# Up weights turned on VectorE in phase A, merges cut in halves, and a shorter LoRA set-up in a one-core AdaLN + FFN kernel

## The reference

```python
# block 0: a per-sample 64x64 mixing, then a linear layer with 8 LoRA adapters summed into it
y  = einsum('bct,bcd->bdt', x, L0_cond_weights[itok_B_0_15])
x1 = x + (y @ W.T + bias + lora_out(y))            # lora: B (scaled by 2*lora_weights) times A, rank 8*16 = 128
# block 1: per-sample adapter of rank 16, then a gated FFN with 4-bit weights
x2 = (x1 @ B[id].T) @ A[id].T
Wg, Wu, Wd = NF4[codes] * scales                    # codes are int32, one scale per 64 inputs
out = x1 + (silu(x2 @ Wg.T) * (x2 @ Wu.T)) @ Wd.T   # hidden size 2752, i.e. 21 chunks of 128 and a tail of 64
```

## Time and profile before

| | us |
|---|---|
| median of 3 runs (1006.99 to 1011.08) | 1008.95 |
| the profiled execution, its own time | 1010.47 |
| its span, first to last instruction | 1008.8 |
| TensorE busy | 987.7 |
| VectorE busy | 878.0 |
| ScalarE busy | 775.0 |

### The profile page before, as it was taken

The page is one execution under the profiler, slowest core; times in us unless marked ns, Lnnn a source line. Parts: engine busy times, 40 slices in busy tenths (PEclk is TensorE's granted clock), DMA queues, the critical chain, the costliest instruction groups (busy, mean ns, idle before and its releaser), DMA issues.

```text
span 1008.8 us, 14537 instructions
## 1 busy us (share of the span) xinstructions
PE 987.7 (98%) x5280; PEld 845.6 (84%) x5280; DVE 878.0 (87%) x853; ACT 775.0 (77%) x929; POOL 231.3 (23%) x269
## 2 busy tenths in 40 slices
PE   4999999999999989999999999999999999999998
PEld 3898889889898868888888888888888888888887
DVE  3899999989999979999999999999999999962353
ACT  4788888878878869988988879888888888853220
POOL 4024533432441221122121211112302122121000
PEclk9999999999999999999999999999999999999999
DMA  9846447347334336866555555656366564564666
GB/s 245 221 139 155 99 110 173 87 104 192 86 93 98 69 58 125 147 116 129 104 101 106 97 101 120 112 105 126 84 122 112 101 120 88 106 136 76 194 221 230
DMA packets 73655, 126.28 MB, mean 125 GB/s; under 512 B 7505, under 2 KB 49505, under 8 KB 73585
## 3 DMA queue, kind: packets, MB, share of 16 engines
q0 software_dynamic: 15200, 51.41, 31.4%
q1 hardware_dynamic: 57056, 72.89, 24.4%
q10 hardware_dynamic: 1328, 1.05, 0.3%
HBM read 66.61 MB, written 67.11 MB: 133 GB/s over the span
## 4 chain that ended last, share of the span: by engine, by line
PE 89%; DVE 8%; DMA 1%; issue 1%; ACT 1%; ACTq 0%; DVEq 0%
PE ps_z L1157 23%; PE ps_y L1157 23%; PE ps_z L1011 13%; PE ps_gu L1136 12%; PE ps_gu L1071 3%; PE ps_t L1071 3%; PE ps_t L1058 3%; DVE val L783 3%; DVE val L785 3%; PE ps_y L998 2%; PE ps_gu L1028 2%; PE ps_t L1020 1%; DMA la<-in_L_ffn_lora_A 1%; DVE val L813 1%; PE ps_z L988 1%
## 5 line engine op out<-in xcount | busy, mean ns | idle before, releaser
L606 ACT ACTIVATE ring<-codes 128x1024 f32<-128x1024 int32 x455 | 456.4, 1053 | 8.7 <-DVE val L785 4.4
L783 DVE TENSOR_TENSOR val<-val,ring 128x1024 f32<-128x1024 f32 x260 | 320.9, 1234 | 18.5 <-ACT ring L606 1.1
L785 DVE SCALAR_TENSOR_TENSOR val<-ring,val 128x1024 f32<-128x1024 f32 x195 | 240.4, 1233 | 10.6 <-ACT ring L606 2.8
L578 POOL DMA_DIRECT2D out<-staged x80 | 69.3, 927 | 263.7 <-ACT staged L732 254.8
L718 ACT ACTIVATE inter<-ps_gu 128x512 f32<-128x512 f32 x88 | 52.6, 598 | 88.6 <-PE ps_gu L1136 88.1
L1011 PE MATMUL ps_z<-we_hi,y_hi 128*128 128x512 f32 x256 | 104.8, 409 | 0.3 <-DVE y_lo L844 0.3
L1011 PE MATMUL ps_z<-we_hi,y_lo 128*128 128x512 f32 x256 | 100.3, 392 | 0.0
L925 DVE TENSOR_TENSOR inter<-ps_gu,inter 128x512 f32<-128x512 f32 x88 | 60.3, 686 | 45.6 <-ACT inter L718 45.2
L1011 PE MATMUL ps_z<-we_lo,y_hi 128*128 128x512 f32 x256 | 100.0, 391 | 0.0
L520 POOL TENSOR_TENSOR st_hi<-ga_f,one 128x128 fp32r<-128x128 f32 x42 | 37.9, 901 | 234.3 <-ACT ga_f L646 234.3
L1157 PE MATMUL ps_z<-wd_late_hi,in_hi 128*128 128x512 f32 x256 | 81.1, 396 | 0.0
(11 more groups left out here) (136 smaller groups left out, 1853.1 us busy)
## 6 DMA issues: line engine op xcount, KB each, us to landing
out<-staged POOLq DMA_DIRECT2D x80, 512.0 KB, 5.5
codes<-in_L_ffn_down_codes SPq DMA_DIRECT2D x21, 512.0 KB, 4.0
xs<-in_x SPq DMA_DIRECT2D x16, 512.0 KB, 3.5
out<-in_L_ffn_bias SPq DMA_DIRECT2D x4, 2048.0 KB, 14.0
out<-xs POOLq DMA_DIRECT2D x16, 512.0 KB, 5.4
ring<-out SPq DMA_DIRECT2D x16, 512.0 KB, 4.4
out<-ring SPq DMA_DIRECT2D x15, 512.0 KB, 2.9
codes<-in_L_ffn_gate_codes SPq DMA_DIRECT2D x12, 512.0 KB, 4.5
```

What stands on the lines that cost most here:

```text
L578: pool.dma_start(out_rows[t * P:(t + 1) * P, :], staged[:, place, :], accum_op=ALU.add).then_inc(acc_out[place], 16)
L606: act.activation(ring[:, (k - 1) % RING, :], codes[:, n % 2, :], ACT.Identity, bias=offset, scale=slope).then_inc(lines, 1)
L783: ins = dve.tensor_tensor(v, v, line, pick)
L785: ins = dve.scalar_tensor_tensor(out=v, in0=line, scalar=add, in1=v, op0=ALU.add, op1=pick)
```

## The change

- `on_dve` is now true also for the up units of chunks 2 to 9: eight units of phase A are turned by VectorE's transpose, and no longer by TensorE and ScalarE. Their codes come by four transfers each. `V_FROM` goes from 12 to 0: `place_scales` places the scales of all chunks, one column block later (`SCALES_JC` 6).
- `STEPS_A` has 8 steps more, one in each of 8 row tiles from t = 4 on, for the 8 transposes.
- Each merge is two instructions of 512 columns. Each half waits for the same half of the merge before it; the counts of `combo` double.
- LoRA: the scaled factor is written into its turned order at once (a copy less); it is copied out of PSUM in plain float32 first (`ad_bt`, called `lbt_f`), and its hi and lo parts are made from that copy. The column blocks 0 and 1 of W get LoRA by two full float32 products each, instead of six fp32r passes each; blocks 2 to 7 as before. Three PSUM tiles are used in the set-up (`ps_w`).
- The last x1 is turned into ps_y and its adapter product goes into ps_z, so these two no longer wait for ps_t. The wait for the last mask (`bx_masked`) moves from the turning of units to the second down product of phase B.

```diff
-        return UNITS[n][0] != "d" and n >= PHASE_A_UNITS
+        return UNITS[n][0] != "d" and (n >= PHASE_A_UNITS or UNITS[n][0] == "u" and 2 <= UNITS[n][1] < 10)
...
-    STEPS_A = [13] * NT
+    STEPS_A = [13] * 3 + [13 + (t % 3 > 0) for t in range(13)]
...
-    SCALES_JC = 5
-    V_FROM = 12
+    SCALES_JC = 6
+    V_FROM = 0
...
-        ps_w = [ps_z, ps_gu]
+        ps_w = [ps_gu, ps_z, ps_y, ps_gu, ps_z, ps_gu, ps_z, ps_gu]
...
+            act.wait_ge(setup_t, 1)
+            act.activation(ad_bt[:, :, :].rearrange("j q p -> j (q p)"), ps_t[:, :], ACT.Copy).then_inc(setup_evac, 1)
             act.wait_ge(lora_a_in, 16)
             act.activation(la_hi, la[:, :], ACT.Copy).then_inc(la_hi_ready, 1)
-            act.wait_ge(setup_t, 1)
-            act.activation(lbt_hi.rearrange("j (p q) -> j q p", q=DC),
-                           ps_t[:, :].rearrange("j (q p) -> j q p", q=DC), ACT.Copy).then_inc(setup_evac, 1)
+            act.wait_ge(setup_evac, 1)
+            act.activation(lbt_hi.rearrange("j (p q) -> j p q", q=DC), lbt_f, ACT.Copy).then_inc(lbt_hi_ready, 1)
...
-                    if op > 1:
-                        dve.wait_ge(combo, COMBOS * n + op - 1)
-                    line = ring[:, (op - 1) % RING, :]
...
+                    for h in range(2):
+                        cols = slice(h * HALF, (h + 1) * HALF)
+                        line, into = ring[:, (op - 1) % RING, cols], v[:, cols]
+                        if op > 1:
+                            dve.wait_ge(combo, 2 * (COMBOS * n + op - 2) + h + 1)
...
+            def add_lora_whole(jc):
+
+                for h in range(2):
+                    ins = pe.matmul(ps_w[jc][:, h * HALF:(h + 1) * HALF], la[:, jc * P:(jc + 1) * P],
+                                    lbt_f[:, h * HALF // DC:(h + 1) * HALF // DC, :], start=False, stop=True)
+                ins.then_inc(we_mm, 1)
...
             def turn_x1(t, turned_before):
                 pe.wait_ge(x1_ready, 2 * (t + 1))
-                wait(pe, evicted, P_NO[turned_before])
-                wait(pe, wd_lo_ready, D_NO[turned_before])
+                if t < NT - 1:
+                    wait(pe, evicted, P_NO[turned_before])
+                    wait(pe, wd_lo_ready, D_NO[turned_before])
```

70 lines of the change are left out of this document (39 added, 31 removed).

## The result

The change makes the kernel slower: the median goes from 1009.46 to 1018.76 us (6 runs each, 1016.88 to 1020.45 after), ratio 1.0089, 95% interval 1.0073 to 1.0106. That lies above the predicted range (997 to 1014). The profiled execution took 1018.35 us, its span is 1016.6, 7.8 more than before; what follows accounts for these 7.8 us. The medians differ by 9.3 us, 1.5 more than the two spans, and that part has no row.

A forecast was written before the change was run, and what follows sets the result against it. VectorE was taken to set phase A's end, TensorE to bound phase B. Start -2.7, work +7.8, waits -4.6 gave +0.5; with -1.8 at the end, -1.3 us: 1009.2 for the profiled execution, median 1007.7, range 997 to 1014.

The forecast's parts named there:

- The set-up: Before phase A: LoRA products start about 5 us sooner, so VectorE starts phase A 2.7 us sooner, bounds 1 and 4.
- But then ScalarE is the late one: Set-up: after the full products end at 16.7 to 20.1, ScalarE's copies decide; first block of W copied at 18 to 19.
- my two prices: Set-up: a full product of 512 columns takes 0.86 us at 2.4 GHz, twice that at 1.2; four take 3.4 to 6.8.
- VectorE's work in phase A: Phase A: eight transposes add 16.8 us, halves add 10.9 and save 19.9, together +7.8 us.
- the 105 places and the 0.06 us: Phase A merges: halves save 0.19 us at each of 105 dependent places and add 0.06 us to each of 182 merges.
- Waits: Phase A: of VectorE's 5.6 us of waiting, 1 us stays, since VectorE is later and TensorE lighter: -4.6 us.
- The end of phase A: Behind the last x1 sum: product 0.3 us sooner, about 1.5 us from less TensorE idling; -1.8 us, bounds 0 and -3.3.
- Phase B: Phase B: halves lighten VectorE but TensorE has no idle time to give back, so 0 us.
- Full price of each half: Phase A merges: halves don't overlap, each merge costs 1.36 us, +29 us, 1037 us in all; chance 0.04.
- VectorE keeps up: Phase A: a merge in halves costs no more than a whole one (1.14 us), time 997.4 us; chance 0.25.
- TensorE's clock: Phase A: TensorE's stops come in lumps that lower its clock four times or more, +8 us or more, 1016; chance 0.11.
- The forecast's own range: Whole kernel: 1003 to 1013 us, from start 1 to 4, end 0 to -3.3, waits 0 to 3, halves +-0.02 us.

The follow-up runs named there:

- light GpSimd: The changed kernel, with GpSimd filling both parts of its phase A splits with a constant (all row tiles but the last for adapter products): 1.0020 of before, 1011.46 us.
- two turns: The changed kernel with two units of phase A (up units of chunks 4 and 8) turned on VectorE instead of eight: 0.9955 of before, 1004.46 us.
- change without turns: The changed kernel with all 26 units of phase A turned on TensorE again and scales placed as before: 0.9947 of before, 1005.17 us.
- halves with the last x1: The kernel before with merges in halves and the last x1 in the banks of y, old LoRA set-up: 0.9973 of before, 1006.95 us.
- LoRA alone: The kernel before with only the new LoRA set-up and the moved wait for the last mask: 1.0008 of before, 1009.78 us.
- plain rows: The kernel with two units turned on VectorE, its LoRA factor copied so full products read consecutive columns: 0.9949 of before, 1004.12 us.

## Why the prediction failed

The reading of what bounds phase A held, and with it the sign of the risk: VectorE sets its end, and the 7 us taken off TensorE were cover. The forecast for the last x1 was +0.5 us, and it was +9.2. Two terms of the sum failed: the set-up, which had the wrong sign, and what the halves save VectorE, which left out GpSimd beside it. By its own steps:

**The set-up, forecast -2.7 us (bounds 1 to 4 sooner), measured +2.75.** This is the largest miss, 5.4 us, and outside its bounds. Three steps of it failed. First, "But then ScalarE is the late one" is wrong: TensorE is. The second block of W landed late (its turn starts at 14.26), which the sum had no term for, the full products took the upper of my two prices (6.9 us for four, of 3.4 to 6.8; the first two for the level, the last two for their stepped read), and they ended at 22.95, where I had 16.7 to 20.1. The first copy of W starts at 19.70 instead of 18 to 19, and the third block only 0.8 us sooner than before (22.95 for 23.73). Second, the scale products are 1.46 us longer, which I had named, but I had called part of that hidden; none was. Third, I looked at the new place of the scales only as TensorE time. That the copies out of ps_y stand behind the next block on ScalarE, and that the first y goes into ps_y, is in the code; it costs the 1.81 us of wait. Sum: -0.8 + 1.5 + 1.8 = 2.5 of the 2.75. Scales placed one block earlier take this back (start 44.69). That the full products came out near my upper price was luck: the last two ran at the full level, and the stepped read, which I had not seen, made them as slow as the lower one.

**VectorE's work in phase A, forecast +7.8, measured +11.5.** The transposes were right: 16.6 us for eight against 16.8. The halves were to save 9.0 (+10.9 - 19.9) and save 6.0 in the merges. The light GpSimd tells the reason: there the merges take 221.0 us, in the change 227.7, before 233.7, of which 3.6 were contention by the same reckoning (63 merges beside GpSimd, 0.04 to 0.11 us longer each). Without it on either side the saving is 230.1 - 221.0 = 9.1, as forecast. So the 105 places and the 0.06 us, of which I was least sure, held up, and what failed is that I priced VectorE's instructions as if nothing ran beside them; the 3 us is what GpSimd's stretched splits cost more than before. The 3.6 us are an estimate; no run has the kernel before with a light GpSimd. Another 1.1 us lie in the scales: seven of them now have a transpose right behind that needs them (0.12 us each), and some are beside GpSimd.

**Waits, forecast -4.6: measured -5.1.** Right. **The end of phase A, forecast -1.8: measured -1.4.** Right in size and in its split: the banks give some 0.3 us, the rest is the fall of the clock that didn't come there. That it didn't come was in part luck, since after stops of the same 1.70 us it came once and once not. **Phase B, 0:** right.

**The rivals.** *Full price of each half*: fell. Neighbours start 0.60 us apart. (The section of the Trainium skill that the prediction sets against this, "The DRAIN you can't avoid" of the page "VectorE: DVE Perf Modes", has the exception itself: a next operation that is not held starts earlier.) These rows of the change show it:

```profile
150.44 0.68 DVE L860 TENSOR_TENSOR xs<-ps_z,xs 128x512 f32<-128x512 f32 x1
151.04 2.48 DVE L792 TENSOR_TENSOR val<-val,ring 128x512 f32<-128x512 f32 x4
```

*VectorE keeps up*: fell. A merge in halves costs 1.20 us, not 1.14, and VectorE sets the end. With two turns TensorE is the bound, but because VectorE has little to do for them, not by this rival's price. *TensorE's clock*: fell as a cause. TensorE did stop, 9.8 us in 7 stops for y_lo, in lumps of up to 2.9, and the clock did fall to 1.2 GHz after two of them. The first, and the two windows that hold the falls:

```profile
287.71 0.50 PE L1026 MATMUL ps_z<-we_hi,y_hi 128*128 128x512 f32 x1 [2.88 <-DVE y_lo L853]
```

```profile
290.00:295.00 5.00, 5.00 (x32) 4.51 (x31) 5.00 (x10) 3.27 (x4) 4.92 (x2) 0.83 0.94 184
...
350.00:355.00 5.00, 5.00 (x21) 4.01 (x21) 4.97 (x8) 2.08 (x3) 4.92 (x3) 0.69 1.02 193
```

But VectorE had 5.00 and 4.97 of 5 us to do in these windows and waited for 0.5 us in all of phase A, so these falls cost nothing. My sign for this rival, a clock below 1.00 in phase A, was a bad one: it came true, and the rival was wrong.

**The chances.** The forecast's own range (1003 to 1013) put 1 to 4 us sooner on the set-up because every edit in it shortened something; a case "the set-up starts phase A later" had no share at all, and all that lies above 1014 had 0.15. With the right +2.75 and the same rest it would have given 1013, and with the 3.7 us of work 1017.

**What stays open.** The change without turns measured 0.9947, while halves with the last x1 give 0.9973 and LoRA alone 1.0008; their product is 0.9981. The three spans (1005.6, 1005.4, 1007.3) don't show such a gap. The profiled execution of the change without turns has a fall of the clock behind the last x1 and is the slowest of its four: 1007.24 us, the others 1005.14 to 1005.17, two of them at a granted clock of 1.000. Four executions with few falls, against the highest median of before (1010.51), could make such a gap; so could a set-up gain that is worth something only with the halves. Nothing here tells them apart. Nor is it shown why the granted clock falls behind the last x1 in some of these kernels and not in others, or why the second block of W lands late with eight units.

## What to carry to other kernels

Two engines that are both nearly full must be read as a pair: work moved from one to the other pays only up to the idle time that the receiver has, and here that room (9.5 us, made by the halves) held two turns of 2.1 us, with 1.5 us of gain in the trace, and not eight. The versions with two turns (0.9949 with plain rows, 1004.12 us) or none (0.9947, 1005.17 us) beat both kernels. When a step is moved in one engine's stream, follow its PSUM tile to the next user and look where the copy that frees it stands on the other engine. And when gaps between dependent instructions are filled, ask which third engine was living in them.
